# A mixture-of-experts kernel: the experts' down product in split operands, over two pieces of 128 rows

## The reference, cut to what matters

```
x = x + layernorm(attention(layernorm(x)))        # x: 4 x 512 x 256, 16 heads of 16
h = layernorm(x)                                  # the second block works on h
hid = h + attention2(rmsnorm(h))                  # 16 heads of 128
x2 = rmsnorm(hid)                                 # 2048 tokens x 256
top_w, top_i = top_k(softmax(x2 @ gate.T), 4)     # 16 experts, 4 for each token, weights made to sum to 1
act = silu(x2 @ w1g[e].T) * (x2 @ w1u[e].T)       # 176 wide, for each chosen expert e
routed = sum over e of top_w * (act @ w2[e].T)    # the down product: 176 -> 256
shared = silu(x2 @ sg.T) * (x2 @ su.T) @ sd.T     # 352 wide, all tokens
x = x + layernorm(hid + routed + shared)
```

## Time and profile before

| | |
|---|---|
| median of 3 runs | 1222.49 us (1221.7 to 1225.82) |
| profiled execution | 1221.95 us, span of the trace 1220.2 us |
| TensorE busy | 1160.6 us, 95% |
| VectorE, ScalarE, GpSimd busy | 846.3, 799.6, 580.7 us |
| granted TensorE clock, mean | 0.99 |
| loop over tiles, first to last scatter | 1000.51 to 1178.92 us |
| scatter (L746) | 79, mean 1.555 us on GpSimd, 3.8 us to landing |

### The profile page before, as it was taken

One profiled execution on the slowest core, in us unless ns is written; L12 is line 12 of the kernel. 1 busy time (PEld: TensorE's weight loads), 2 busy tenths in 40 slices (PEclk: granted clock), 3 DMA queues, 4 the chain that ended last, 5 costly groups with the idle time before them and its releaser, 6 DMA issues.

```text
span 1220.2 us, 25017 instructions
## 1 busy us (share of the span) xinstructions
PE 1160.6 (95%) x7868; PEld 988.4 (81%) x7868; DVE 846.3 (69%) x2663; ACT 799.6 (66%) x2069; POOL 580.7 (48%) x844
## 2 busy tenths in 40 slices
PE   6999999899999999999999999999998879999986
PEld 5766566689999989999989999889986769999962
DVE  5778888576677667876677876668865755555535
ACT  3587888677778776778776787777786524444422
POOL 4063655454334444457343466334453446666650
PEclk9999999999999999999999999999999989999998
DMA  8965555256631211213121131211114237777766
GB/s 271 284 190 168 173 175 170 89 176 191 189 114 57 91 51 57 81 53 123 35 69 37 35 109 67 69 36 54 64 54 132 78 112 116 118 119 118 119 110 223
DMA packets 111779, 139.58 MB, mean 114 GB/s; under 512 B 11364, under 2 KB 94820, under 8 KB 111524
## 3 DMA queue, kind: packets, MB, share of 16 engines
q1 hardware_dynamic: 97204, 119.10, 32.2%
q0 software_dynamic: 14448, 18.88, 9.5%
HBM read 63.36 MB, written 61.87 MB: 103 GB/s over the span
## 4 chain that ended last, share of the span: by engine, by line
PE 76%; DVE 8%; ACT 6%; issue 4%; POOL 3%; DMA 2%; SPq 1%; POOLq 0%; ACTq 0%; DVEq 0%
PE bank L1500 56%; PE bank L1742 5%; PE bank L1926 5%; PE bank L1561 2%; DVE bank L1127 2%; PE bank L1597 2%; PE bank L1614 2%; POOL xs_rows L684 1%; PE bank L1604 1%; PE bank L1905 1%; PE bank L1936 1%; ACT pT L842 1%; POOL sum_rows L746 1%; ACT p L966 1%; DVE hs L1358 1%
## 5 line engine op out<-in xcount | busy, mean ns | idle before, releaser
L1127 DVE CUSTOM_DVE_ANT_0 bank<-bank,mask 128x512 f32<-128x512 f32 (+3 forms) x512 | 235.1, 522 | 42.3 <-PE bank L1500 21.6
L957 ACT ACTIVATE p<-bank,stat 128x512 f32<-128x512 f32 (+3 forms) x256 | 131.6, 527 | 127.0 <-DVE stat L1127 127.0
L537 POOL CAST w_hl<-raw_qkv 128x512 fp32r<-128x512 f32 x96 | 58.8, 613 | 301.9 <-DMA raw_qkv<-in_qkvo 154.2
L1500 PE MATMUL bank<-xT,w_hl 128*128 128x512 f32 x768 | 190.3, 396 | 0.0
L1500 PEld LDWEIGHTS bank<-xT,w_hl 128*128 128x128 f32 x768 | 142.2, 188 | 37.1 <-issue 2.0
L746 POOL DMA_INDIRECT sum_rows<-mid,goal x79 | 122.9, 1555 | 70.7 <-DVE mid L1464 68.1
L966 ACT ACTIVATE p<-p,stat 128x512 f32<-128x512 f32 (+3 forms) x256 | 123.1, 553 | 14.7 <-DVE stat L1361 14.7
L538 POOL TENSOR_TENSOR w_hl<-raw_qkv,w_hl 128x512 fp32r<-128x512 f32 x96 | 124.2, 1294 | 7.8
L1383 DVE TENSOR_TENSOR o<-bank,o 128x512 fp32r<-128x512 f32 x64 | 44.2, 690 | 109.4 <-ACT o L973 109.4
L1500 PE MATMUL bank<-pT,v 128*128 128x256 f32 (+2 forms) x576 | 117.1, 348 | 0.0
L1500 PE MATMUL bank<-k,q 128*128 128x512 f32 (+2 forms) x576 | 111.5, 337 | 2.5 <-ACT pT L950 1.7
(11 more groups left out here) (248 smaller groups left out, 2561.3 us busy)
## 6 DMA issues: line engine op xcount, KB each, us to landing
raw_qkv<-in_qkvo SPq DMA_DIRECT2D x32, 768.0 KB, 5.3
xs_rows<-blank SPq DMA_DIRECT2D x32, 520.0 KB, 3.3
xs_rows<-blank SPq DMA_DIRECT2D x5, 2730.0 KB, 14.6
xrow<-xs_rows SPq DMA_DIRECT2D x79, 130.0 KB, 2.5
raw_o<-in_qkvo SPq DMA_DIRECT2D x32, 256.0 KB, 3.6
sum_rows<-blank SPq DMA_DIRECT2D x3, 2176.0 KB, 8.5
stk<-xT SPq DMA_DIRECT2D x96, 64.0 KB
stk<-k_hl SPq DMA_DIRECT2D x96, 64.0 KB
```

Of the source, the lines that this page charges most:

```text
L537: link(pool.tensor_copy(hi, raw))
L957: act.activation(p2[:, n % 2, POFF[qi]:POFF[qi + 1]], s2(t), ACT.Exp, scale=-1.0, bias=stat2[:, 0, n % 2, t:t + 1], accum_out=stat2[:, 1, ...
L1127: return dve.tensor_tensor_reduce(scores, scores, mask[:, TB - scores.shape[1]:], scale=-1.0, scalar=-2.0 * MASKED, op0=ALU.add, op1=ALU.m ...
L1500: ins = pe.matmul(out, a, b, start=start and i == 0, stop=stop and i == len(pairs) - 1, **kw)
```

## The change

The 176 rows of an expert's w2 are cut into a first piece of 128 and a rest of 48. The first piece is held as high and low part (`w2a`, three products). The rest is laid out as one operand of 128 rows: partitions 0 to 63 hold its rounded rows, partitions 64 to 127 their remainders (`w2b`; of each 64 rows 48 count, and h is zero at the other 16). VectorE writes h to `hx` with the last 48 columns twice, so that h turned has the same layout. The high and low part of h (`ht_hi`, `ht_lo`) times `w2b` give the rest in two products, five in all. Plain fp32 is no longer used there.

Around it:
- SP loads the first pieces of quarter 3 where it loaded w2r's, then waits for the end of the shared experts and loads all rests, each twice, before tile 4.
- ScalarE rounds `w2a` by quarters (`round_a`, after steps 4, 9 and 10 of the shared experts and in round 0); GpSimd subtracts for its low part (`rest_a`: quarter 0 between two steps of `shared_lo`, the others after the sends) and rounds the upper half of `w2b` (`round_b`); ScalarE and VectorE make the lower half (`copy_b`, `rest_b`; the first quarter before the loop, the others in rounds 1, 4 and 7).
- The scaling of the down product into `yt` moves from VectorE to ScalarE, ahead of the copy of h turned. VectorE gets the low part of h turned instead.
- The turned x (`xtt`) gets a buffer of its own. Some semaphores are shared (`x_in` is now `part_in`, `e_x` and `t_in` are now `rows_in`).

```diff
--- before.py
+++ after.py
@@
-    H2E = EI // 2
+    EA, EB = P, EI - P
...
-            w2r = sb(late, "w2r", [H2E, E, 2, D])
+            w2a = sb(late, "w2a", [P, E, 2, D], F32R)
...
-            ht = sb(loops, "ht", [H2E, 2, 2 * P])
+            w2b = sb(loops, "w2b", [P, E, D], F32R)
+            hx = sb(loops, "hx", [P, 2, 2 * P])
+            ht_hi = sb(loops, "ht_hi", [P, 2, 2 * P], F32R)
+            ht_lo = sb(loops, "ht_lo", [P, 2, 2 * P], F32R)
+            xtt = sb(loops, "xtt", [P, 2, 2, D], F32R)
...
+        W2_POOL = (3, 5, 7, 8)
...
+        def down_pieces(first, count):
+
+            done = 0
+            while done < count:
+                k, p = (first + done) // P, (first + done) % P
+                m = min(P - p, count - done)
+                yield moe_d[k // MGC, p:p + m, k % MGC, 2 * C * P:], done, m
+                done += m
+
+        def pieces_a(q):
+            return [(e, *piece) for e in range(E // B * q, E // B * (q + 1))
+                    for piece in down_pieces(SHI + e * EI, EA)]
+
+        def pieces_b(q):
+            return [(e, src, half * P // 2 + first, m) for e in range(E // B * q, E // B * (q + 1))
+                    for half in range(2) for src, first, m in down_pieces(SHI + e * EI + EA, P // 2)]
...
@@ SyncE: load_w2, load_tile and the order of the loads
-                for e in range(E // B * q, E // B * (q + 1)):
-                    for h, g, k, p, first, m in down_pieces(e):
-                        sp.dma_start(w2r[first:first + m, e, h, :], moe_d[g, p:p + m, k, 2 * C * P:])\
-                            .then_inc(w2_in[q], 16)
+                for e, src, first, m in pieces_a(q):
+                    sp.dma_start(w2a_raw[first:first + m, e, 1, :], src).then_inc(w2a_in[q], 16)
...
                 if i >= NX:
                     sp.wait_ge(e_y, i - NX + 1)
+                    sp.wait_ge(e_goal, i - NX + 1)
...
             load_w2(B - 1)
+            sp.wait_ge(f_dn, SHARED)
+            for q in range(B):
+                for e, src, first, m in pieces_b(q):
+                    sp.dma_start(w2b_raw[first:first + m, e, :], src).then_inc(part_in[q], 16)
             for i in range(NX // 2, NT):
                 load_tile(i)
@@ GpSimd
+            def rest_a(q):
+                own = block_of(q)
+                pool.wait_ge(w2a_round, q + 1)
+                pool.tensor_tensor(w2a[:, own, 1, :], w2a_raw[:, own, 1, :], f32(w2a[:, own, 0, :]), ALU.subtract)\
+                    .then_inc(w2_pool, 1)
+
+            def round_b(q):
+                own = block_of(q)
+                pool.wait_ge(part_in[q], 16 * (1 + len(pieces_b(q))))
+                pool.tensor_copy(w2b[0:P // 2, own, :], w2b_raw[0:P // 2, own, :]).then_inc(w2_pool, 1)
+
             for s in range(1, LO_POOL):
                 shared_lo(s)
+                if s == 4:
+                    rest_a(0)
             for j in range(TPB):
                 send_tile(B - 1, j)
+            rest_a(1)
+            round_b(0)
+            rest_a(2)
+            round_b(1)
+            rest_a(3)
 
             for i in range(NT):
+                if i in (2, 4):
+                    round_b(i // 2 + 1)
+                pool.wait_ge(e_goal, i + 1)
                 pool.wait_ge(e_y, i + 1)
@@ ScalarE
+            def round_a(q):
+                own = block_of(q)
+                act.wait_ge(w2a_in[q], 16 * len(pieces_a(q)))
+                act.activation(w2a[:, own, 0, :], w2a_raw[:, own, 1, :], ACT.Copy).then_inc(w2a_round, 1)
+
+            def copy_b(q):
+                act.wait_ge(part_in[q], 16 * (1 + len(pieces_b(q))))
+                if q:
+                    act.wait_ge(w2b_rest, q)
+                act.activation(w2b_hi[P // 2:, :, :], w2b_raw[P // 2:, block_of(q), :], ACT.Copy).then_inc(w2b_copy, 1)
...
+                if s in (4, 9, 10):
+                    round_a((4, 9, 10).index(s))
...
+            copy_b(0)
+            for i in range(NT + 2):
...
+                if i >= 2:
+                    m = i - 2
+                    act.wait_ge(e_dn, m + 1)
+                    if m >= NY:
+                        act.wait_ge(y_sent[m % NY], 16 * (m // NY))
+                    act.activation(yt[:, m % NY, :], bank[6 + m % 2][:, 0:D], ACT.Copy,
+                                   scale=xt[:, m % NX, D + 1:D + 2]).then_inc(e_y, 1)
+                if 1 <= i <= NT:
                     act.wait_ge(e_ht, i)
-                    if i >= 3:
-                        act.wait_ge(e_dn, i - 2)
-                    act.activation(ht[:, (i - 1) % 2, :], bank[4 + (i - 1) % 2][0:H2E, 0:2 * P], ACT.Copy).then_inc(e_htc, 1)
+                    act.activation(ht_hi[:, (i - 1) % 2, :], bank[4 + (i - 1) % 2][:, 0:2 * P], ACT.Copy)\
+                       .then_inc(e_htc, 1)
                 if i + 2 < NT:
                     take_x(i + 2)
+                if i == 0:
+                    round_a(B - 1)
+                if i in (1, 4, 7):
+                    copy_b((1, 4, 7).index(i) + 1)
@@ VectorE
+            def rest_b(q):
+                dve.wait_ge(w2b_copy, q + 1)
+                dve.tensor_tensor(w2b[P // 2:, block_of(q), :], w2b_raw[P // 2:, block_of(q), :],
+                                  f32(w2b_hi[P // 2:, :, :]), ALU.subtract).then_inc(w2b_rest, 1)
...
-                    dve.tensor_tensor(sl[:, i % 2, :], sl[:, i % 2, :], bank[i % 2][:, EI:2 * EI], ALU.mult)\
+                    both = [P, 2, EB]
+                    dve.tensor_tensor(hx[:, i % 2, 0:EA], sl[:, i % 2, 0:EA], bank[i % 2][:, EI:EI + EA], ALU.mult)
+                    dve.tensor_tensor(hx[:, i % 2, EA:].rearrange("p (a n) -> p a n", a=2)[:, :, 0:EB],
+                                      sl[:, i % 2, EA:].unsqueeze(1).to_broadcast(both),
+                                      bank[i % 2][:, EI + EA:2 * EI].unsqueeze(1).to_broadcast(both), ALU.mult)\
                        .then_inc(e_h, 1)
...
-                    dve.tensor_scalar(yt[:, m % NY, :], bank[6 + m % 2][:, 0:D], xt[:, m % NX, D + 1:D + 2], None,
-                                      ALU.mult).then_inc(e_y, 1)
+                                      spare[:, :], ALU.min).then_inc(e_goal, 1)
+                if 1 <= i <= NT:
+                    dve.wait_ge(e_htc, i)
+                    dve.tensor_tensor(ht_lo[:, (i - 1) % 2, :], bank[4 + (i - 1) % 2][:, 0:2 * P],
+                                      f32(ht_hi[:, (i - 1) % 2, :]), ALU.subtract).then_inc(e_htl, 1)
                 if i + 2 < NT:
                     take_x(i + 2)
+                if i in (1, 4, 7):
+                    rest_b((1, 4, 7).index(i) + 1)
@@ TensorE: down(i)
-                pe.wait_ge(e_htc, i + 1)
+                    pe.wait_ge(w2_pool, W2_POOL[i // (E // B)])
+                    pe.wait_ge(w2b_rest, i // (E // B) + 1)
+                pe.wait_ge(e_htl, i + 1)
...
-                for h in range(2):
-                    ins = pe.matmul(bank[6 + i % 2][:, 0:D], ht[:, i % 2, P * h:P * (h + 1)],
-                                    w2r[:, ds(expert[i], 1), h, :].rearrange("p a n -> p (a n)"),
-                                    start=h == 0, stop=h == 1)
-                ins.then_inc(e_dn, 1)
+                first, last = slice(0, EA), slice(EA, 2 * P)
+                a_hi, a_lo = (w2a[:, ds(expert[i], 1), part, :].rearrange("p a n -> p (a n)") for part in (HI, LO))
+                product(bank[6 + i % 2][:, 0:D],
+                        [(ht_hi[:, i % 2, first], a_hi), (ht_lo[:, i % 2, first], a_hi), (ht_hi[:, i % 2, first], a_lo),
+                         (ht_hi[:, i % 2, last], w2b[:, ds(expert[i], 1), :].rearrange("p a n -> p (a n)")),
+                         (ht_lo[:, i % 2, last], w2b[:, ds(expert[i], 1), :].rearrange("p a n -> p (a n)"))])\
+                    .then_inc(e_dn, 1)
```

More of the change, by code:

```diff
@@ L84, in sandwich_kernel @@
         hs = sb(ctx, "hs", [P, T, D])
+        with ExitStack() as late_raw:
+            w2a_raw = sb(late_raw, "w2a_raw", [P, E, 2, D])
         with ExitStack() as late:
-            w2r = sb(late, "w2r", [H2E, E, 2, D])
+            w2a = sb(late, "w2a", [P, E, 2, D], F32R)
         xT = sb(ctx, "xT", [P, B, 2, C, TB], F32R)
@@ L201, in sandwich_kernel @@
         yt = mid
-        xtt = sh_hi[:, :, :].rearrange("p r n -> p (r n)")[:, 0:4 * D].rearrange("p (i a n) -> p i a n", i=2, a=2)
         mask_f = xn_mid[:, 0:2, :].rearrange("p j d -> p (j d)")
-        x_in = [sem(f"x_in{b}") for b in range(B)]
+        part_in = [sem(f"part_in{b}") for b in range(B)]
         w1_in = sem("w1_in"); small_in = sem("small_in")
@@ L242, in sandwich_kernel @@
         w_in = [sem(f"w_in{c}") for c in range(C)]; w_hi = sem("w_hi"); w_lo = sem("w_lo")
-        w2_in = [sem(f"w2_in{q}") for q in range(B)]
+        w2a_in = [sem(f"w2a_in{q}") for q in range(B)]
+        w2a_round = sem("w2a_round"); w2b_copy = sem("w2b_copy"); w2_pool = sem("w2_pool"); w2b_rest = sem("w2b_rest")
+        W2_POOL = (3, 5, 7, 8)
```

(39 more changed lines are left out.)

22 lines of the change are left out of this document (10 added, 12 removed).

## The result

The changed kernel takes 1255.88 us (median of 4 runs, 1253.14 to 1256.94), beside 1222.1 (1219.64 to 1225.82) for the kernel before, timed beside it: a ratio of 1.027, 95% interval 1.0239 to 1.0301. It is slower, as forecast, but by 34 us where 17 were forecast, and outside the range. The profiled execution took 1255.99 us (span 1254.2), 34.0 more than the 1221.95 of before.

The account below looks back on a forecast made before the run. After the change a ring of waits, not TensorE's work, was to bound the loop. Terms 15.2 + 2.4 + 1.2 + 1.6 + 0.4 - 4 = +16.8 us on 1221.95 gave 1238.8, median 1239; range 1228 to 1246.

Parts of the forecast that it names:

- SP: 39 more transfers ahead of tile 4: In SP's queue between tiles 3 and 4: 39 more pieces at 0.39 each delay tile 4 by 15.2 us (13 to 17).
- remainder of w2a in the ranking: GpSimd's new 1024-column remainder stalls VectorE's ranking of experts, delaying the row sends: +2.4 us (0 to 2.5).
- half clock after tile 4: TensorE, idle before tile 4, restarts with about three us at half speed: +1.2 us (0 to 1.7).
- the round in the loop: Routed experts' loop: 2.22 a round against 2.273 gives back 4 us over 74 rounds.
- remainders of w2b: VectorE's 1024-column remainders in rounds 4 and 7 cost 0.8 each: +1.6 us (0 to 2.4).
- last rounds, end: Last three rounds go from 1.95 to 2.2, less 0.4 for a shorter last product and write of y: +0.4.
- I price the 16- and 64-row ones alike.: SP's issue ahead of tile 4: a piece's row count hardly matters, so every w2b piece costs 0.39 us.
- the bound of 0.43: Upper bound on SP's issue price per piece ahead of tile 4; the lower was 0.33, together 13 to 17 us.
- The ring decides: 2.22.: Loop: product, y, ht_hi, ht_lo and hand-overs in series take 2.22 a round, above TensorE's own 2.00 (2.09 after a wait).
- a longer ring: Loop: ScalarE's second wait adds 0.05 to 0.1, or w2b's conversions block VectorE and GpSimd: 1241 to 1250; chance 0.15.
- The rival of the other side: Loop: TensorE stays the bound, one-pass matmuls take 0.108, a round 1.95, 24 us come back: 1217; chance 0.03.

Follow-up runs that it names:

- experiment 7: Changed kernel with w2b's 64- and 48-row pieces cut into pieces of at most 32 rows: 1263.58 us, 7.7 more than the changed kernel.
- experiment 1: Changed kernel with TensorE's load of the next expert number moved behind the up product, ahead of down's wait: 1247.69 us, steady round 2.243.
- experiment 5: Kernel before, with only TensorE's load of the next expert number moved behind the up product: 1220.38 us, ratio 1.0002 to before.
- experiment 10: Changed kernel, loop kept: w2b's first two quarters and w2a's last loaded early, tiles 0-7 first, later remainders on VectorE, one per round: 1226.83 us.

## Why the prediction was wrong, step by step

| step of the forecast | forecast | measured |
|---|---|---|
| SP: 39 more transfers ahead of tile 4 | +15.2 | +22.9 |
| remainder of w2a in the ranking | +2.4 | +2.4 |
| ahead of the ranking | 0 | -0.5 |
| half clock after tile 4 (measured: tile 4 to the second scatter, net of the shorter product) | +1.2 | +1.0 |
| GpSimd's hand-over from y to the scatter | 0 | +0.5 |
| the round in the loop (measured: the 67 steady rounds) | -4 | +3.6 |
| remainders of w2b (measured: all of the seven early rounds) | +1.6 | +3.1 |
| last rounds, end | +0.4 | +1.0 |
| sum | +16.8 | +34.0 |

The loop's +6.7 is split at the ninth scatter; 0.4 of the 3.1 is the longer round, seven times.

*"I price the 16- and 64-row ones alike."* This step was mis-sized. The twelve pieces of before cost 0.39 each whatever their rows, but the pieces of w2b cost 0.47 with their gap, and 0.64 when one of 64 rows, of which there are 20, stands ahead; even the bound of 0.43 was too low. The mechanism (SP's queue ahead of tile 4, and nothing in TensorE's work to cover it) was right, and experiment 7 shows that the price goes by transfers. The kernel is slower, as forecast, by this term; the loop, which was to give back 4, went the other way. The Trainium skill ("DMA: Bandwidth & Descriptors", Anatomy of one DMA) puts the sequencer's dispatch of a transfer at about 50 ns and calls the generation of descriptors small; that table is for GpSimd's transfers, and SP's rows here show 0.42 to 0.60 us, eight to twelve times as much.

*"The ring decides: 2.22."* The ring was summed rightly: 2.24 with the sequencer out of the way (experiment 1), and 2.24 in the last three rounds, which load no more from the table. The step that failed is what it was compared with. I took TensorE to be bound either by its work or by the ring. There is a third loop, down's release, down, the transposes, the fetch from the table, up, and back to down: 1.37 to up's first weights and 0.92 to 0.95 to down's, 2.29 to 2.32. It cost nothing while TensorE's sequencer ran ahead, and it came into being with the wait. I named the wait that the change adds but not what is queued behind it on TensorE. The Trainium skill ("Perfetto Trace Analysis", Sequencer-only Instruction) says that an instruction which the sequencer executes itself waits for its semaphores in the sequencer, and that nothing behind it is decoded meanwhile; the traces of experiments 1 and 5 agree with that. The rival "a longer ring" (1241 to 1250, 0.15) had the direction but another cause.

*The remainder in the ranking* went as written, VectorE's 2.46 and 2.4 in the chain against a forecast of 2.4. *The half clock* lasted 6.3 us, from 1025.85 to 1032.2, not three. The three were a misreading: the two windows of the earlier trace rows show only a part of the low clock, and in the kernel before TensorE worked under it for 5.3 us, from 991.47 to 996.8. Up to the second scatter it cost more than the forecast: the same stretch takes 5.32 here and 3.46 in experiment 10, which has the same loop and a granted clock of 1.00 there, so 1.9; it nets to 1.0 since the new product is shorter. It went on into the third round. *The remainders of w2b* cost nearly twice as much: the rounds in which they stand come also under GpSimd's copies, and the first of them under the half clock; the parts weren't told apart. *GpSimd's hand-over* was not in the sum. Ahead of a scatter GpSimd's list now has a wait for goal beside the one for y; whether this makes the 0.5, no run tells.

*The last rounds* were taken at 2.2 and are 2.24. The rival of the other side (a one-pass matmul of 0.108) fell: in the changed kernel the five matmuls of down are 0.12 apart.

## What to carry to other kernels

When a change makes an engine wait that ran ahead until now, list all that its sequencer does behind that wait, scalar loads and address arithmetic too, and sum the loop from one release to the next; a hidden fetch becomes a link as soon as the engine is held. Cut all the loops that are close to each other before you judge one: here one edit gave 6 us in the loop, another 2, and both 15. Moving many small transfers ahead of the one that someone waits for costs their number times the issue price of that very form, so load what is not needed yet behind what is, or in an earlier stage, and convert it no sooner than the round before its use.

## What had not been expected of the hardware

- SP's issue of a transfer takes 0.58 to 0.60 us when the one ahead of it has 64 rows x 1 KB, whatever rows it has itself (16, 32, 48 and 64 all occur), and 0.41 to 0.49 behind one of 16 to 48 rows, but for one of 0.32. The seven of w2a ahead of them, 32 to 128 rows, take 0.37 to 0.43 but for one of 0.79. The price does not simply rise with the rows; why 64 should be dearest, no run here tells.
- A fetch from SBUF into a register of TensorE's sequencer takes 0.30 us, with 0.15 and 0.02 of checks behind it, and from down's release to the next product's weights it adds 0.08 us a round, though 0.47 long, since some of it lies under the transposes.
